# Normalised rows centred, scaled and split on GpSimd, and the value projection as products of 128 columns

## What is computed

```python
def _layernorm(x, axis=-1, eps=1e-05):
    m = jnp.mean(x, axis=axis, keepdims=True)
    v = jnp.var(x, axis=axis, keepdims=True)
    return (x - m) / jnp.sqrt(v + eps)

h = tok_ref(x, ...)                        # embed, 3 graph layers: 784 x 64 an image
h = jnp.concatenate([h, txt], axis=1)      # 861 rows of 64 an image
h = h + attn_ref(_layernorm(h), ...)       # q, k, v = x @ W.T + b; 4 heads of 16; softmax
h = h + ffn_ref(_layernorm(h), ...)        # shared MLP + 2 of 4 experts by a gate
return h
```

## Time and profile before

| | us |
|---|---|
| median of three runs | 5057.14 (5054.25 to 5059.23) |
| profiled execution, its own time | 5066.99 |
| its span in the trace | 5065.2 |
| PE busy | 4809.6 (95%) |
| DVE busy | 3530.6 (70%) |
| ACT busy | 2990.7 (59%) |
| POOL busy | 1272.2 (25%) |

### The profile page before, as it was taken

One profiled execution on the slowest core, in us unless ns is written; L12 is line 12 of the kernel. 1 busy time (PEld: TensorE's weight loads), 2 busy tenths in 40 slices (PEclk: granted clock), 3 DMA queues, 4 the chain that ended last, 5 costly groups with the idle time before them and its releaser, 6 DMA issues.

```text
span 5065.2 us, 81302 instructions
## 1 busy us (share of the span) xinstructions
PE 4809.6 (95%) x29710; PEld 3201.2 (63%) x29710; DVE 3530.6 (70%) x7660; ACT 2990.7 (59%) x6161; POOL 1272.2 (25%) x1169
## 2 busy tenths in 40 slices
PE   6699999999999999999999999999999999999997
PEld 5466666666666666666656666666666666666654
DVE  4477667777777777777677777777767677777774
ACT  0156566666566566566656556666656666656665
POOL 3122222222222222223222222222223222222221
PEclk8699999999999999999999999999999999999998
DMA  2433323333433332333332333332333333332220
GB/s 87 106 72 76 85 78 78 85 71 76 87 79 78 85 73 78 86 81 77 84 70 75 84 80 78 86 72 74 87 83 79 80 82 71 79 85 69 40 47 6
DMA packets 193397, 386.00 MB, mean 76 GB/s; under 512 B 74986, under 2 KB 118634, under 8 KB 193002
## 3 DMA queue, kind: packets, MB, share of 16 engines
q1 hardware_dynamic: 191978, 379.91, 33.3%
q10 hardware_dynamic: 1024, 0.89, 0.1%
HBM read 309.13 MB, written 109.26 MB: 83 GB/s over the span
## 4 chain that ended last, share of the span: by engine, by line
PE 55%; issue 23%; POOL 10%; DVE 6%; ACT 3%; DMA 2%; POOLq 0%; SPq 0%; ACTq 0%; DVEq 0%; another core or an unknown queue 0%
PE ps L1225 9%; PE ps L1204 8%; PE ps L1213 8%; PE ps L1257 8%; PE ps L1275 5%; PE ps L1248 4%; PE ps L1318 3%; DVE neg_max_halves L977 3%; POOL tokens L829 3%; POOL moe_T L824 2%; ACT probs L861 2%; PE ps L1339 2%; PE ps L364 1%; POOL nodes_T L806 1%; DMA image_rows<-image_by_row 1%
## 5 line engine op out<-in xcount | busy, mean ns | idle before, releaser
L977 DVE TENSOR_REDUCE neg_max_halves<-ps 123x1 f32<-123x432 f32 (+1 forms) x3584 | 2014.6, 597 | 602.6 <-PE ps L1225 592.9
L861 ACT ACTIVATE probs<-ps 123x432 f32<-123x432 f32 x3584 | 1684.0, 541 | 603.3 <-PE ps L1204 580.4
L1225 PE MATMUL ps<-k_stack,q_stack 96*123 96x432 f32 x3584 | 1302.3, 397 | 35.7 <-DMA k_stack<-qk_scratch 21.6
L1204 PE MATMUL ps<-q_stack,k_stack 97*123 97x432 f32 x3584 | 1246.8, 394 | 63.9 <-DVE neg_max_halves L977 22.1
L1225 PEld LDWEIGHTS ps<-k_stack,q_stack 96*123 96x123 f32 x3584 | 646.7, 188 | 431.6 <-issue 290.3
L1204 PEld LDWEIGHTS ps<-q_stack,k_stack 97*123 97x123 f32 x3584 | 642.8, 186 | 359.0 <-issue 96.2
L1213 PE MATMUL ps<-probs,v_and_one 123*32 123x432 f32 x7168 | 787.8, 553 | 14.0 <-ACT probs L861 14.0
L924 ACT ACTIVATE hidden<-ps,plain_w 128x432 f32<-128x432 f32 x640 | 400.2, 634 | 181.0 <-PE ps L1275 180.9
L1257 PE MATMUL ps<-adjacency,parts_hi 112*128 112x392 f32 x1344 | 466.1, 347 | 5.1 <-DVE parts_lo L999 4.1
L1257 PE MATMUL ps<-adjacency,parts_lo 112*128 112x392 f32 x1344 | 459.9, 342 | 0.0
L359 POOL COPY patch_columns<-image_rows 96x392 f32<-96x392 f32 x256 | 243.2, 978 | 845.0 <-PE ps L364 756.2
(11 more groups left out here) (157 smaller groups left out, 6115.3 us busy)
## 6 DMA issues: line engine op xcount, KB each, us to landing
image_rows<-image_by_row SPq DMA_DIRECT2D x256, 586.9 KB
q_stack<-qk_scratch SPq DMA_DIRECT2D x256, 216.0 KB, 7.9
k_stack<-qk_scratch SPq DMA_DIRECT2D x256, 216.0 KB, 9.3
image_by_row<-in_x SPq DMA_DIRECT2D x192, 196.0 KB
qk_scratch<-parts_hi SPq DMA_DIRECT2D x64, 432.0 KB, 2.5
qk_scratch<-parts_lo SPq DMA_DIRECT2D x64, 432.0 KB, 3.1
out<-tokens SPq DMA_DIRECT2D x64, 215.2 KB
tokens_next<-in_txt SPq DMA_DIRECT2D x64, 19.2 KB
```

The source lines that it names most:

```text
L861: act.activation(P[:, (g * 2 * NB + unit) % SLOTS, h, :], T[0:BLK, 0:HW], ACT.Exp, scale=SCALE).then_inc(free[r], 1)
L977: v.tensor_reduce(NM[:, qb * HEADS + h, half:half + 1], T[0:BLK, 0:keys], AX.X, ALU.max, negate=True).then_inc(free[r], 1)
L1204: mm = pe.matmul(T[0:BLK, 0:cn], KS[:, g % 2, h, kb * BLK:(kb + 1) * BLK], QS[:, g % 2, h, c0:c0 + cn], start=True, stop=True)
L1225: mm = pe.matmul(T[0:BLK, 0:cn], QS[0:SHIFT_ROW, g % 2, h, qb * BLK:(qb + 1) * BLK], KS[0:SHIFT_ROW, g % 2, h, c0:c0 + cn], start=True, st ...
```

## The change

It has three parts.

1. `ln`, `scale`, `hi` and `lo` of both normalisations go from DVE to POOL. DVE keeps `sum`, `mean`, `var` and its share of `ln2`. `mean_ready` replaces `rstd_ready`; `sum` of the next image now waits for POOL's `centred`, and POOL's `ln` waits for its own last `lo`.
2. `v` becomes two steps, of blocks 0 to 3 and of blocks 4 to 6, each with a bank of its own. A block's stack is multiplied once with 128 columns, high and low weights side by side (`vsplit`, filled at the start). DVE adds bias and high half, then the low half: two instructions a step in place of one an image.
3. The tables of places are set anew.

```diff
-MAX = ((-0.693, 0.158), (-0.638, 0.167))
-FINISH = ((1.016, 1.084), (1.072, 1.145))
...
+MAX = ((-0.694, 0.158), (-0.638, 0.168))
+FINISH = ((0.995, 1.063), (0.994, 1.097))
...
+VALUE = (-0.952, -0.989)
...
+VGAP = 0.154
...
-            + [(g + VALUE[b], ("v", g)), (g + STORE[b], ("store", g))])
+            + [(g + VALUE[b], ("v", g, 0)), (g + VALUE[b] + VGAP, ("v", g, 1)), (g + STORE[b], ("store", g))])
```

```diff
+                    elif kind == "ln":
+                        _, g, which = st
+                        counted(pool, mean_ready, nth, ("mean", g, which))
+                        counted(pool, normed, nth, lo_last[st])
+                        pool.tensor_tensor(XN[:, :, 0, :], rows_of(g, which),
+                                           st7[which][:, 0, :].unsqueeze(2).to_broadcast([BLK, NB, HID]), ALU.subtract
+                                           ).then_inc(centred, 1)
                     elif kind == "ln2":
                         stats = st7[st[2]]
                         counted(pool, var_ready, nth, st)
-                        pool.tensor_tensor(stats[:, 3, :], stats[:, 2, :], halfneg[:, :], ALU.pow).then_inc(rstd_ready, 1)
+                        done(pool.tensor_tensor(stats[:, 3, :], stats[:, 2, :], halfneg[:, :], ALU.pow), st)
+                    elif kind == "scale":
+                        rstd = st7[st[2]][:, 3, :].unsqueeze(2).to_broadcast([BLK, NB, HID])
+                        need(("ln2", *st[1:]))
+                        done(pool.tensor_tensor(XN[:, :, 0, :], XN[:, :, 0, :], rstd, ALU.mult), st)
+                    elif kind == "hi":
+                        need(("scale", *st[1:]))
+                        filled(pool, turn, xt_last[st])
+                        done(pool.tensor_copy(XHL[:, :, 0, :], XN[:, :, 0, :]), st)
+                    elif kind == "lo":
+                        need(("hi", *st[1:]))
+                        pool.tensor_tensor(XHL[:, :, 1, :], XN[:, :, 0, :], XHL[:, :, 0, :].bitcast(F32),
+                                           ALU.subtract).then_inc(normed, 1)
...
                         v.wait_ge(full[r], n)
                         v.tensor_tensor(HT[:, c], T[:, 0:GHALF], dinv[:, c], ALU.mult).then_inc(free[r], 1)
-                    elif kind in ("sum", "mean", "ln"):
+                    elif kind == "sum":
                         _, g, which = st
-                        b, p = g % 2, g // 2
-                        src = HN[p % 2][:, :, b, :] if which == "a" else H[:, :, b, :]
-                        mean = st7[which][:, 0, :]
-                        if kind == "sum":
-                            if which == "a":
...
                     elif kind == "v":
-                        b = st[1] % 2
+                        _, g, part = st
+                        ks = blocks_of(part)
+                        k, kn = slice(ks[0][0], ks[-1][0] + 1), len(ks)
                         v.wait_ge(full[r], n)
-                        v.tensor_tensor(
-                            VV[:, b, :, :, 0:HD],
-                            T[0:BLK, 0:NB * HID].rearrange("p (k h d) -> p k h d", h=HEADS, d=HD),
-                            row("bv").rearrange("p (h d) -> p h d", h=HEADS).unsqueeze(1)
-                            .to_broadcast([BLK, NB, HEADS, HD]), ALU.add).then_inc(free[r], 1)
+                        two = T[0:BLK, 0:kn * 2 * HID].rearrange("p (k a h d) -> p k a h d", a=2, h=HEADS, d=HD)
+                        bias = row("bv").rearrange("p (h d) -> p h d", h=HEADS).unsqueeze(1).to_broadcast([BLK, kn, HEADS, HD])
+                        done(v.tensor_tensor(VV[:, g % 2, k, :, 0:HD], two[:, :, 0, :, :], bias, ALU.add), st)
+                        need(st)
+                        v.tensor_tensor(VV[:, g % 2, k, :, 0:HD], two[:, :, 1, :, :], VV[:, g % 2, k, :, 0:HD], ALU.add
+                                        ).then_inc(free[r], 1)
...
                         _, g, half, kb = st
                         if (half, kb) == (0, 0):
-                            emptied(pe, turn, ("v", g))
+                            emptied(pe, turn, ("v", g, 0))
+                            emptied(pe, turn, ("v", g, 1))
...
+                    elif kind == "v":
+                        for k, at in blocks_of(st[2]):
+                            mm = pe.matmul(T[0:BLK, at * 2 * HID:(at + 1) * 2 * HID],
+                                           XS["a"][:, k * BLK:(k + 1) * BLK], vsplit[:, :], start=True, stop=True)
```

93 lines of the change are left out of this document (38 added, 55 removed).

## The result

The changed kernel takes 4942.9 us, median of 4 runs (4939.7 to 4946.5), and the kernel before 5058.2 (5054.3 to 5065.9, 4 runs). The ratio is 0.977, with a 95% interval of 0.9754 to 0.9787. That is 115 us less; the forecast was 89 less, and 4942.9 lies in its range. The profiled execution of the changed kernel took 4939.7 us with a span of 4937.9, against 5067.0 and 5065.2 before, so the two traces differ by 127 us. The 31 full patterns of two images explain all of it: their mean was 150.63 us and is 146.52.

The account below looks back on a forecast made before the run. PE was taken as the engine to watch, losing time in waits. Terms: -1.4 + 0.7 - 1.8 - 0.75 + 0.4 = -2.85 us a pattern, -88 over 31 patterns, so 5057 becomes 4968 us; range 4870 to 5060.

Parts of the forecast that it names:

- term 3: Even image's attention rows: with the offload PE reaches the transposes 11.4 us after the mean, not 13.3; gain 1.8 us.
- Term 1: Value projection on PE: seven products of 128 columns replace 14, saving 0.7 us an image, 1.4 a pattern.
- Term 2: Value steps in their new place: the even image's saved 0.7 us is lost again in PE's waits for DVE.
- Term 4: Even image's expert rows: PE's 0.49 us wait for a maximum and the slow start behind it go, gain 0.75 us.
- Term 5: Odd image's attention and expert rows cost nothing; even-image gate steps on DVE meeting POOL's work cost PE 0.4 us a pattern.
- the first rival: Even image's attention rows: POOL's chain is no limit, or the clock no longer falls there; 4900 to 4840 us, chance 0.2.
- Slower than before: POOL and DVE get in each other's way in the even image's gate: +2.35 us a pattern, 5130 us, chance 0.14.

Follow-up runs that it names:

- the longer chain: The changed kernel with the rounding of the even image's attention rows made three times over on POOL: 4991.8 us.
- six partial kernels: The kernel before with value projection, offload or new table alone (5060.1, 5069.7, 5333.4 us), or two of these three (5020.0, 5258.9, 5095.5 us).

## Why the prediction was right, step by step

The sign and the range held, and the forecast of 4968 lay 25 us above the result. Several of its terms were still off, and nearly all of these misses point one way, to too small a gain. That the time still lies near the sum is partly luck: PE has new waits for ACT, 0.5 and 0.35 us, that no term holds, and the terms as measured overlap, since the 2.7 us of term 3 hold time at the lower clock. They do not add up to the 4.1 us of a pattern.

- **Term 1, -1.4 us on PE: right.** The value steps took 2.95 us of PE a pattern and take 1.31, so 1.64. Changed kernel against the one with the old value form: 147.9 - 146.3 = 1.6 in patterns without a fall of the clock.
- **Term 2, +0.7 lost in waits for DVE: wrong for this place, right as a mechanism.** In the new places nothing is lost. In the old places all is lost (the value projection alone: 5060), mostly at the odd image, where I had put nothing, and not at the even one. The step that failed is the assumption that seven maxima in a row would hold PE up. The even image's second value step waits 0.5 us, but for ACT's exponentials, which the kernel with the old form also waits for.
- **Term 3, -1.8: the offload does shorten this stretch, the size is 2.7, and the wait for POOL is wrong.** The transposes come 10.55 us behind the mean in place of 13.26, and up to 1.6 of the difference are the clock, which the term did not hold. The sum for POOL's chain was 11.4 because centring and scaling were put at 1.14 and the rounding at 0.95 by the nearest rows, while they take 0.94, 0.94 and 0.56. The chain ends 0.2 us before PE is there, so the expected wait of PE for POOL does not exist.
- **Term 4, -0.75: the wait went, the gain is smaller.** PE's 0.49 us for a maximum there is gone. In the same stretch the second value step and the score product behind it wait 0.54 and 0.35 us for ACT. The transposes come 10.7 us behind the mean, and POOL's last step ends 1.1 us ahead of them where 0.7 had been estimated.
- **Term 5, 0 and +0.4: the 0 is right, the 0.4 not visible.** Both odd chains end well before their transposes, 1.9 and 2.4 us in the median. Two gate subtractions on DVE did become slower, 344 to 634 ns and 448 to 712, which is what the term feared, but neither mean reached 1 us, and the first gate subtraction went from 518 to 183. No wait of PE follows them.
- **Left out: the graph's wait.** PE's wait for POOL's node scaling, 0.8 us in each pattern before, is not in any term. It is gone in all four kernels with the whole new table (4 times left in each) and there 34 times in all kernels with the offload and old places. So the new order is enough to remove it. It is not the only way: the value projection alone, in old places, has it 5 times. Why is not shown; with both edits in old places PE loses the same time behind the value products and still has this wait 34 times.
- **The mechanism that came true is the first rival's.** It said that POOL's chain is no limit, or that the clock no longer falls there, and the prediction's own sign for it was that PE shows no wait for POOL. Both happened: no such wait once a pattern, and a clock of 1.00 over the stretch. The time is still in the forecast's range and not at 4900 to 4840. The rival's sum was also wrong by its own terms: 2.85 + 1.6 + 1.5 to 3.5 is 6.0 to 8.0 us a pattern, not 5 to 7.
- **The clock was left out of the forecast.** Before, 30 of 31 patterns had a fall, now 10 have, and 4.8 us a pattern at the lower clock became 1.25. What that is worth is bounded and not settled. In the changed kernel a pattern with a fall takes 147.8 us against 146.3; by that price it is 1.5 of the 4.1 us gained. In the kernel before and with the value projection alone, where PE often waits for DVE anyway, the difference is 0.6 (150.3 against the single pattern of 149.7; 150.8 against 150.2), which makes it 0.6. The prediction had put the clock wholly into a rival with 0.2. Taking a wait away can buy clock too, and putting one in costs it, as the longer chain shows; but the value projection alone got the clock back without a shorter pattern.
- **Slower than before: its mechanism did not show.** Gate instructions blocked by POOL cost PE nothing that can be seen. What does make this change slower is another order: of the six partial kernels four are slower than the kernel before, one is equal and one faster.

The step that fails as a method is the costing of places. I read the new order and summed POOL's chain in it, which was right, but I took what is fixed by the old order as the base for everything else. The sum -2.85 then names offload and value projection as the earners. The runs show that in the old order these edits earn nothing.

## What to carry to other kernels

When a change moves work between engines and resets the order as well, price the edit in the old order, the order alone, and both, before giving a term to one of them; here they are +38, +275 and -115 us. Time saved on the busiest engine, by less work or by a higher clock, is only time where the engine next to it is ahead: look which release the next instruction waits for, and when it came, before the saving is counted. A chain that is moved to a slower engine is judged by its last step against the reader's arrival (0.2 us here), and what stands between its steps counts as well as how long each takes: the expert bias between them costs 107 us here, a rounding made three times 49.

## What the runs showed of the hardware

- On POOL an operation on 123x448 fp32 values with one operand broadcast over 64 values takes 0.94 us (centring, scaling), with two full operands 1.14 to 1.16, and a rounding copy 0.57. I had expected 1.14 for the first and 0.95 for the last. On DVE the same centring and rounding take 0.62 and 0.43 us in the median of the kernel before, so the move costs a factor of 1.3 to 1.5. The longest there, beside POOL's work, took 1.55 and 1.10.
- Products of 64 and of 128 columns, each with new stationary values of 128x123, start 0.104 and 0.106 us apart, save the first pair of a group at 0.03 and 0.06. That the loading of the stationary values sets the pace is my reading of it; no run changed their size.
- A single fall of the clock of 3.4 us costs 1.4 to 1.5 us of a pattern in the changed kernel, and 0.6 in the kernel with the value projection alone. With a wait of PE of 1 to 2 us put in at the transposes, 15 and 27 of 31 patterns have a fall where 10 had one, so the same order of work has it in some patterns and not in others.
